# Sparse products of a graph network on one Trainium2 core: a 16-slot gather ring, static index columns, loops of four groups

## The chip, the cores and the metric

The kernel runs on 1 core of one Trainium2 chip. The metric is device time of that core in microseconds: three runs of the kernel before gave 11555.72, 11559.22 and 11560.43 us, median 11559.22 us. One more execution was profiled; all rows below are from it.

## The reference, cut to what matters

Four graph layers run one after the other on 50000 nodes of 128 features and 25000 edges sorted by destination. The change is in the second (L1), which is five sublayers, each with five sparse products on top of one another:

```python
def prop(z):
    return segment_sum(edge_weight[:, None] * z[src], dst, num_segments=N_SUP)
for i in range(5):
    z = h @ W[i] + b[i]
    x_start = prop(z)
    xi = h
    for _ in range(5):
        xi = (prop(xi) + x_start) / (2.0 + GAMA)
    mean, var = jnp.mean(xi, axis=0), jnp.var(xi, axis=0)
    out = gamma[i] * (xi - mean) / jnp.sqrt(var + BN_EPS) + beta[i]
    h = jnp.where(out > 0, out, 0.01 * out)
```

All of its pixels belong to segment 0, so only one row of the result is used in the end; the products still run over all edges. The kernel folds `x_start` into the others, so that there are 5 products in each of 5 sublayers: 25 passes over the edges.

## The kernel before, in words

The 25000 edges are 200 tiles (`T`) of 125 edges, one edge to a partition, partition 0 being kept for a carried sum. Four tiles are a group (`GR`), two groups a half-and-half turn of a loop (`U` = 8 tiles, `IT` = 25 turns). A pass works on a table in HBM that has one row of 128 floats for each edge position, reads it by index, and writes the next pass's table.

For each tile of a pass:
- **GpSimd (POOL)** gathers 128 rows of 512 bytes into slot `j` of `G` by an indirect DMA (L864 in `l1_gather`). `G` has 8 slots. The index column comes from `ridx`, 8 columns that VectorE refills from `gidx` (L936). Each gather carries a wait on the semaphore `s_go`, which has been up since the program's start (`steady`), and at every fourth tile there is a wait on `l_idx` (the columns are there) and on `l_sum` (the group that used these four slots two groups ago has been summed).
- **TensorE (PE)** makes the row of the last, unfinished segment of the tile (L981, a matmul with one column of `lring`), and after VectorE's carry the segment sums of the tile (L995, the mask `M` as weights and `G` as data).
- **VectorE (DVE)**, once per group: the carried row goes through the four tiles in five short operations (`running_sums`, L354 and L356), then `lring` and `ridx` are refilled (L934, L936), the four masks of the next group are made (`edge_mask`, L377), and the group's sums are added to the constant part and left in `Y` (L948). In the last pass of a sublayer (`k == 4`) it copies the sums to `Y` and squares them instead (L943, L945).
- **SyncE (SP)** stores each group of `Y` to the next table (L849, `l1_store`, not in a last pass).
- **ScalarE (ACT)** works only in the last passes (L956), in which PE also makes the transposed sums (L991) and the sums over nodes (L962, L964 in `node_sums`).

The order is set by the engines' own programs and by semaphores. PE's group `g` starts when group `g-1`'s carry (`l_ch`) and mask are there and its gathers have landed (`l_got[j]`, one semaphore for each slot). POOL starts a pass only when all stores of the pass before have landed (`l_tab`). Between two sublayers is a dense stage (`turn_act`, `turn_dve`, `turn_pe`), about 139 us, in which POOL gathers nothing. The sublayer loop is `over_layers`: sublayer 0 is written out, sublayers 1 to 4 are a loop; the programs of the five passes in it are written out one behind the other.

The prediction also speaks of two other places where POOL issues gathers: L397 (first graph layer) and L803 (positions, `PGOT`).

Of the kernel before, what the change touches and what calls it, by code (L numbers as in the profile page):

```python
# [7 lines left out]
P, D = 128, 128  # L31
# [6 lines left out]
TG = T // 2  # L38
TP = T + U
# [14 lines left out]
def build(nc, x0, src, dst, ea, ew, w0, b0, w1, b1, gamma, beta, w2, b2, we, be, coef, linw, linb, asrc, adst, out):  # L54
    assert T * TE == E and IT * U == T and CHUNKS * NJ == NC_ and CHUNKS % 2 == 0
# [30 lines left out]
    with ctx:  # L86
# [39 lines left out]
        G = sb("G", [P, U, D + HEADS])  # L126
# [666 lines left out]
        def positions(pool, c, s, n):  # L793
# [28 lines left out]
        l_w, l_wr, l_col, l_base, l_idx, l_mask, l_lr, l_ch, l_row, l_sum, l_ev, l_xt, l_xc, l_yl, l_sq = (  # L822
            sem("l_" + n) for n in "w wr col base idx mask lr ch row sum ev xt xc yl sq".split())
        l_got = pool_sems("l_got", U)
# [9 lines left out]
        def rounds(l, k):  # L834

            return (l * NL + k) * IT
# [15 lines left out]
        def l1_gather(pool, l, k):  # L852
            r0 = rounds(l, k)
            steady(pool, 16 * rounds(l, k + 1))
            for h in range(2):
                pool.wait_ge(l_tab[h], 16 * rounds(l, k + 1))
            with pool.Fori(0, IT) as i:
                for j in range(U):
                    g = 2 * (r0 + i) + j // GR
                    steady(pool, g + 1)  # L860
                    if j % GR == 0:
                        pool.wait_ge(l_idx, g + 1)
                        pool.wait_ge(l_sum, g + 1)
                    pool.indirect_dma_start(G[:, j, 0:D], None, tab_in(k), bass.IndirectOffsetOnAxis(  # L864
                        ap=ridx[:, j:j + 1], axis=0)).then_inc(l_got[j], 16)
# [58 lines left out]

        def l1_dve(dve, l, k):
            r0 = rounds(l, k)
            last = k == NL - 1
            with dve.Fori(0, IT) as i:
                for h in range(2):
                    g = 2 * (r0 + i) + h  # L930
                    running_sums(dve, g, U * i + GR * h, h, lambda j: G[0:1, j, 0:D],
                                 lambda jj: PS[0:1, CAR, jj, :], carry[:, 0:D], l_row, l_ch)

                    nc.vector.tensor_copy(lring[:, GR * h:GR * h + GR],  # L934
                                          lastc[:, bass.ds(U * i + U + GR * h, GR)]).then_inc(l_lr, 1)
                    nc.vector.tensor_copy(ridx[:, GR * h:GR * h + GR],  # L936
                                          gidx[:, bass.ds(U * i + U + GR * h, GR)]).then_inc(l_idx, 1)
                    for j in range(GR):
                        ins = edge_mask(U * i + GR * (h + 1) + j, GR * (1 - h) + j, wccol)
                    ins.then_inc(l_mask, 1)  # L940
                    dve.wait_ge(l_sum, g + 3)
                    if last:
                        nc.vector.tensor_copy(group_of(Y, h), PS[:, SUM + h, :, :]).then_inc(l_yl, 1)  # L943
                        dve.wait_ge(l_yl, 2 * (IT * l + i) + h + 1)
                        nc.vector.tensor_tensor(SQ[h][:], group_of(Y, h), group_of(Y, h), ALU.mult).then_inc(l_sq, 1)  # L945
                    else:
                        dve.wait_ge(l_tab[h], 16 * (rounds(l, k + 1) + i))
                        nc.vector.tensor_tensor(group_of(Y, h), PS[:, SUM + h, :, :], zt_group(i, h),  # L948
                                                ALU.add).then_inc(l_ev, 1)
# [17 lines left out]
        def l1_pe(pe, l, k):  # L967
            r0 = rounds(l, k)
            last = k == NL - 1
            with pe.Fori(0, IT) as i:  # L970
# [925 lines left out]
```

## Time and profile before

| | us |
|---|---|
| median of three runs | 11559.22 |
| span of the profiled execution | 11598.4 |
| the 25 passes, with the four dense stages between (1326 to 9024) | 7698 |
| busy: PE, DVE, POOL, ACT | 7734.7, 6797.1, 7123.4, 1197.8 |
| granted TensorE clock, mean | 0.659 of 2.4 GHz |

For the profiled execution the page gives the span, from its first to its last instruction, and no time beyond it; the span is 39.2 us (0.34%) longer than the median of the three runs. Durations below are of that one execution and are summed against 11598.4. In a row of the time line the columns are: start in us from the span's beginning, duration in us, engine, line, operation, tiles, count; in brackets the engine's idle time before it and what ended that. "issue" is time in which an engine waited for nothing that the profile shows. For a gather the bar is the time of POOL's own work on it, not the transfer, whose landing has a line of its own.

### The profile page before, as it was taken

The numbers are of one execution on the slowest core, as the hardware profiler recorded it, in microseconds if no ns is written. First come the engines' busy times: TensorE is split into PE (matmuls) and PEld (weight loads), VectorE is DVE, ScalarE is ACT, GpSimd is POOL, SyncE is SP. The second block draws the span as 40 slices with busy tenths as digits, with TensorE's granted clock in tenths as the row PEclk, the third lists the DMA queues.
The fourth block names the chain that finished last, engine by engine and source line by source line (L and its number), as shares of the span: only waits on it lengthen the run. The fifth ranks groups of instructions, "written<-read, shape, count | busy, mean of one in ns | idle before, by whom it ended". The sixth has DMA issues, their size and how long they took to land. (4 is left out here: it accounts for less than half of the span.)

```text
span 11598.4 us, 175759 instructions
## 1 busy us (share of the span) xinstructions
PE 7734.7 (67%) x38121; PEld 5090.7 (44%) x38121; DVE 6797.1 (59%) x24532; ACT 1197.8 (10%) x2596; POOL 7123.4 (61%) x7294
## 2 busy tenths in 40 slices
PE   4633377788777797777877778877779177660090
PEld 2423233357333475333663345743337055560070
DVE  5644655567555576555665556765556666450176
ACT  0122000001000011000010000100000511440005
POOL 5756366663666664666636666456666466766664
PEclk8755555679555697555785556965559578785555
DMA  3133354432444424444334444244543522662106
GB/s 126 44 126 142 91 91 92 92 70 69 92 92 92 90 49 95 91 92 92 61 76 93 92 92 81 58 95 92 91 93 52 178 62 63 174 174 36 24 28 268
DMA packets 1057829, 1076.56 MB, mean 93 GB/s; under 512 B 193805, under 2 KB 913982, under 8 KB 1057648
## 3 DMA queue, kind: packets, MB, share of 16 engines
q0 software_dynamic: 211200, 395.39, 22.0%
q1 hardware_dynamic: 723504, 525.23, 14.3%
q10 hardware_dynamic: 123072, 155.41, 4.3%
q14 instruction: 42, 0.34, 0.0%
q8 instruction: 11, 0.18, 0.0%
HBM read 565.26 MB, written 522.63 MB: 94 GB/s over the span
## 5 line engine op out<-in xcount | busy, mean ns | idle before, releaser
L864 POOL DMA_INDIRECT G<-tab,ridx x5000 | 4746.3, 949 | 3013.2 <-issue 2328.4
L981 PE MATMUL PS<-G,lring 128*1 128x128 f32 x10000 | 2411.0, 361 | 1504.0 <-DMA G<-tab,ridx 1470.1
L356 DVE SCALAR_TENSOR_TENSOR G<-G,whole,PS 1x128 f32<-1x128 f32 (+1 forms) x4050 | 1353.8, 334 | 2568.5 <-PE PS L981 1977.4
L995 PE MATMUL PS<-G,M 128*128 128x128 f32 x10000 | 2780.8, 418 | 45.5 <-DVE G L356 44.0
L995 PEld LDWEIGHTS PS<-G,M 128*128 128x128 f32 x10000 | 2155.6, 274 | 684.6 <-issue 376.4
L981 PEld LDWEIGHTS PS<-G,lring 128*1 128x1 f32 x10000 | 556.1, 85 | 3071.0 <-DMA G<-tab,ridx 2721.0
L377 DVE TENSOR_SCALAR M<-keyrow,keycol,wccol 128x128 f32 (+1 forms) x5004 | 1393.6, 350 | 1.0
L956 ACT COPY big<-PS 128x512 f32 x250 | 146.4, 585 | 7147.2 <-PE PS L991 7147.2
L688 ACT ACTIVATE big<-big,nb,rs 128x128 f32<-128x128 f32 x1564 | 614.8, 479 | 935.4 <-POOL nb L679 911.8
L948 DVE TENSOR_TENSOR Y<-PS,big 128x512 f32<-128x512 f32 x1000 | 679.4, 679 | 0.0
L356 DVE SCALAR_TENSOR_TENSOR carry<-G,whole,PS 1x128 f32<-1x128 f32 (+1 forms) x1350 | 451.2, 334 | 182.0 <-DVE G L356 0.3
L354 DVE COPY G<-carry 1x128 f32<-1x128 f32 (+1 forms) x1350 | 397.8, 295 | 236.9 <-PE PS L981 220.9
L991 PE MATMUL PS<-M,G 128*128 128x128 f32 x2000 | 484.8, 327 | 0.0
L773 PE MATMUL PS<-ones,big 128*128 128x1 f32 (+1 forms) x782 | 171.8, 353 | 361.4 <-ACT big L688 361.4
L991 PEld LDWEIGHTS PS<-M,G 128*128 128x128 f32 x2000 | 328.7, 206 | 101.9 <-issue 37.7
L962 PE MATMUL PS<-ends,Y 128*128 (+1 forms) x2040 | 357.1, 245 | 2.9 <-DVE HT L945 2.9
L1738 PE MATMUL PS<-ident,AL 128*100 128x128 f32 x8 | 2.0, 426 | 520.8 <-DVE AL L1684 520.8
L773 PEld LDWEIGHTS PS<-ones,big 128*128 128x128 f32 (+1 forms) x782 | 169.2, 331 | 364.1 <-ACT big L688 364.1
L962 PEld LDWEIGHTS PS<-ends,Y 128*128 128x128 f32 x2040 | 320.6, 198 | 3.3 <-DVE HT L945 3.3
L660 DVE BATCH_NORM_STATS2 st<-big 128x6 f32<-128x128 f32 x1564 | 314.6, 278 | 4.2
L397 POOL DMA_INDIRECT G<-in_x,ridx x200 | 208.2, 1041 | 156.0 <-DVE ridx L467 93.7
L676 POOL TENSOR_TENSOR rs<-rs,minus_half 128x13 f32<-128x13 f32 (+1 forms) x124 | 297.4, 2399 | 10.3
(387 smaller groups left out, 9973.5 us busy)
## 6 DMA issues: line engine op xcount, KB each, us to landing
tab<-Y SPq DMA_DIRECT2D x1250, 256.0 KB, 3.1
G<-tab,ridx POOLq DMA_INDIRECT x5000, 3.3
big<-agg SPq DMA_DIRECT2D x90, 832.0 KB, 6.4
x<-big ACTq DMA_DIRECT2D x60, 832.0 KB, 3.6
big<-x SPq DMA_DIRECT2D x60, 832.0 KB, 4.8
xt_d<-big ACTq DMA_DIRECT2D x30, 858.0 KB, 7.7
x2n<-big ACTq DMA_DIRECT2D x30, 838.5 KB, 3.5
big<-x2n SPq DMA_DIRECT2D x30, 838.5 KB, 5.3
```

The source lines that it names most:

```text
L354: nc.vector.tensor_copy(row0(j), carried).then_inc(made, 1)
L356: nc.vector.scalar_tensor_tensor(carried if jj == GR else row0(j), row0(j - 1), whole[0:1, bass.ds(tile + jj - 1, 1)], local(jj - 1), ALU. ...
L377: return nc.vector.tensor_scalar(M[:, slot, :], keyrow[:, bass.ds(t * P, P)], keycol[:, bass.ds(t, 1)], weights[:, bass.ds(t, 1)], ALU.is_ ...
L660: ins = nc.vector.bn_stats(st6[0:np_, j, :], V[0:np_, j, :])
L688: ins = nc.scalar.activation(X[0:np_, j, 0:D], V[0:np_, j, :], ACT.Identity, scale=rs[0:np_, s, j:j + 1], bias=nb[0:np_, s, j:j + 1])
L773: ins = nc.tensor.matmul(PS[:, ACC1, 0, 0:1], XN[s][0:np_, j, :], ones[0:np_, 0:1], start=False, stop=False, skip_group_check=True)
L864: pool.indirect_dma_start(G[:, j, 0:D], None, tab_in(k), bass.IndirectOffsetOnAxis(ap=ridx[:, j:j + 1], axis=0)).then_inc(l_got[j], 16)
L948: nc.vector.tensor_tensor(group_of(Y, h), PS[:, SUM + h, :, :], zt_group(i, h), ALU.add).then_inc(l_ev, 1)
L962: nc.tensor.matmul(PS[:, ACC1, 0, 0:2], Y[:, GR * h + j, :], here, start=False, stop=False, skip_group_check=True)
L981: nc.tensor.matmul(PS[0:1, CAR, j % GR, :], lring[:, j:j + 1], G[:, j, 0:D], start=True, stop=True).then_inc(l_row, 1)
L991: ins = nc.tensor.matmul(PS[:, PA + h, j % GR, :], G[:, j, 0:D], M[:, j, :], start=True, stop=True)
L995: ins = nc.tensor.matmul(PS[:, SUM + h, j % GR, :], M[:, j, :], G[:, j, 0:D], start=True, stop=True)
```

## The change

`G` gets 16 slots (`RG`). A pass's 200 gathers are written out (no loop on POOL), each with its own constant column of `gidx`; `ridx`, its refill and `l_idx` go. POOL waits once in 8 gathers, from the 16th on: for the sums of both groups whose slots come next (`l_sum`) and for their carries (`l_ch`). The other 7 gathers of the 8 carry no wait. The loops of PE and DVE have four groups in a turn, 12 turns and two groups written out behind them. The two credits on `l_sum` go, so DVE waits for `g + 1` instead of `g + 3`, which is the same group.

```diff
+RG = 16
+NG = RG // GR
+LI = T // RG
+LREM = (T - LI * RG) // GR
-        G = sb("G", [P, U, D + HEADS])
+        G = sb("G", [P, RG, D + HEADS])
-        l_got = pool_sems("l_got", U)
+        l_got = pool_sems("l_got", RG)
...
         def l1_gather(pool, l, k):
-            r0 = rounds(l, k)
+            g0 = 2 * rounds(l, k)
             steady(pool, 16 * rounds(l, k + 1))
             for h in range(2):
                 pool.wait_ge(l_tab[h], 16 * rounds(l, k + 1))
-            with pool.Fori(0, IT) as i:
-                for j in range(U):
-                    g = 2 * (r0 + i) + j // GR
-                    steady(pool, g + 1)
-                    if j % GR == 0:
-                        pool.wait_ge(l_idx, g + 1)
-                        pool.wait_ge(l_sum, g + 1)
-                    pool.indirect_dma_start(G[:, j, 0:D], None, tab_in(k), bass.IndirectOffsetOnAxis(
-                        ap=ridx[:, j:j + 1], axis=0)).then_inc(l_got[j], 16)
+            for t in range(T):
+                if t >= RG and t % U == 0:
+                    free = g0 + (t - RG) // GR + 2
+                    steady(pool, free, OPS * free + 1)
+                    pool.wait_ge(l_sum, free)
+                    pool.wait_ge(l_ch, OPS * free + 1)
+                pool.indirect_dma_start(G[:, t % RG, 0:D], None, tab_in(k), bass.IndirectOffsetOnAxis(
+                    ap=gidx[:, t:t + 1], axis=0)).then_inc(l_got[t % RG], 16)
...
+        def group_loop(eng):
+            with eng.Fori(0, LI) as i:
+                for q in range(NG):
+                    yield i, q
+            for q in range(LREM):
+                yield LI, q
+
+        def got_before(l, k, slot):
+            return (LI + (1 if slot < GR * LREM else 0)) * (NL * l + k)
...
         def l1_dve(dve, l, k):
-            with dve.Fori(0, IT) as i:
-                for h in range(2):
-                    g = 2 * (r0 + i) + h
-                    running_sums(dve, g, U * i + GR * h, h, lambda j: G[0:1, j, 0:D],
-                                 lambda jj: PS[0:1, CAR, jj, :], carry[:, 0:D], l_row, l_ch)
+            for i, q in group_loop(dve):
+                h, g, tile = q % 2, g0 + NG * i + q, RG * i + GR * q
+                running_sums(dve, g, tile, 0, lambda j, q=q: G[0:1, GR * q + j, 0:D],
+                             lambda jj: PS[0:1, CAR, jj, :], carry[:, 0:D], l_row, l_ch)
...
-                    nc.vector.tensor_copy(ridx[:, GR * h:GR * h + GR],
-                                          gidx[:, bass.ds(U * i + U + GR * h, GR)]).then_inc(l_idx, 1)
...
-                    dve.wait_ge(l_sum, g + 3)
+                dve.wait_ge(l_sum, g + 1)
...
         def l1_pe(pe, l, k):
-            with pe.Fori(0, IT) as i:
-                for h in range(2):
-                    g = 2 * (r0 + i) + h
+            for i, q in group_loop(pe):
+                h, g, tile = q % 2, g0 + NG * i + q, RG * i + GR * q
...
-                        pe.wait_ge(l_got[j], 16 * (r0 + i) + 16)
+                    pe.wait_ge(l_got[s], 16 * (got_before(l, k, s) + i) + 16)
...
-                credit(l_sum, 2)
-                nc.vector.tensor_copy(ridx[:], gidx[:, 0:U]).then_inc(l_idx, 2)
```

The instructions of PE and DVE for a group are otherwise the same, on the same tiles. No other stage of the kernel is touched.

## Rows read from the trace of the kernel before

**Rows 1.** The page: the span, and the gathers of the 25 passes.

```profile
span 11598.4 us, 175759 instructions
...
L864 POOL DMA_INDIRECT G<-tab,ridx x5000 | 4746.3, 949 | 3013.2 <-issue 2328.4
```

**Rows 2.** Busy time by stretch: a middle pass, a last pass, a dense stage.

```profile
core 0: us, PE busy (x) PEld busy (x) DVE busy (x) ACT busy (x) POOL busy (x), PEclk, DMA share, GB/s
...
1613.10:1897.50 284.40, 217.57 (x800) 112.49 (x800) 168.02 (x600) 0.00 (x0) 188.72 (x200) 0.58 0.49 92
...
2467.70:2755.90 288.20, 270.23 (x2020) 232.31 (x2020) 202.52 (x656) 29.27 (x50) 189.55 (x201) 0.92 0.27 46
2755.90:2894.80 138.90, 97.88 (x800) 93.12 (x800) 100.11 (x154) 38.08 (x50) 0.56 (x1) 0.97 0.33 95
```

**Rows 3.** Time line of POOL: gathers 1, 8, 9 and 13 of the first pass.

```profile
1326.48 0.96 POOL L864 DMA_INDIRECT G<-tab,ridx  x1 [125.42 <-issue]
...
1335.24 0.94 POOL L864 DMA_INDIRECT G<-tab,ridx  x1 [0.30 <-issue]
1337.37 0.98 POOL L864 DMA_INDIRECT G<-tab,ridx  x1 [1.18 <-PE PS L995]
...
1342.40 0.94 POOL L864 DMA_INDIRECT G<-tab,ridx  x1 [0.30 <-issue]
```

**Rows 4.** Time line of POOL: the first pass's last gather, and three later heads.

```profile
1600.79 0.94 POOL L864 DMA_INDIRECT G<-tab,ridx  x1 [0.30 <-issue]
1613.10 0.94 POOL L864 DMA_INDIRECT G<-tab,ridx  x1 [11.37 <-issue]
...
2894.84 0.99 POOL L864 DMA_INDIRECT G<-tab,ridx  x1 [138.37 <-issue]
...
8735.39 0.94 POOL L864 DMA_INDIRECT G<-tab,ridx  x1 [10.63 <-issue]
```

**Rows 5.** Time line of all engines, 1760 to 1773: one turn of the ring.

```profile
1761.82 0.94 POOL L864 DMA_INDIRECT G<-tab,ridx  x1 [0.90 <-PE PS L995]
...
1765.57 0.94 POOL L864 DMA_INDIRECT G<-tab,ridx  x1 [0.30 <-issue]
...
1768.93 0.38 PE L981 MATMUL PS<-G,lring 128*1 128x128 f32 x2 [0.61 <-DMA G<-tab,ridx]
...
1769.91 1.71 PE L995 MATMUL PS<-G,M 128*128 128x128 f32 x6 [0.19 <-DVE G L356]
...
1772.42 0.94 POOL L864 DMA_INDIRECT G<-tab,ridx  x1 [0.70 <-issue]
```

**Rows 6.** The gathers' line by itself: durations in ns, landing.

```profile
L864 POOL DMA_INDIRECT G<-tab,ridx x5000: 938/945/1473, 1326.5 to 9009.6; - x193
...
DMA to landing us min/median/max: 2.9/3.3/5.5
```

**Rows 7.** Time line, 1590 to 1595: two carries of DVE with gathers nearly in time.

```profile
1590.54 0.34 DVE L356 SCALAR_TENSOR_TENSOR carry<-G,whole,PS 1x128 f32<-1x128 f32 x1
...
1592.82 0.38 PE L981 MATMUL PS<-G,lring 128*1 128x128 f32 x2 [0.20 <-DMA G<-tab,ridx]
...
1594.79 0.33 DVE L356 SCALAR_TENSOR_TENSOR carry<-G,whole,PS 1x128 f32<-1x128 f32 x1
```

**Rows 8.** Time line, 2604 to 2611, in a last pass: PE's row matmuls of two groups.

```profile
2605.40 1.03 PE L981 MATMUL PS<-G,lring 128*1 128x128 f32 x8
...
2610.28 0.82 PE L981 MATMUL PS<-G,lring 128*1 128x128 f32 x6
```

**Rows 9.** Other gathers of POOL, by shape: busy us, mean ns, idle before.

```profile
L803 POOL DMA_INDIRECT PGOT<-lastpos,PIDX x200 | 237.1, 1186 | 76.0 <-issue 51.9 <-POOL PIDX L798 23.8 <-DMA PGOT<-lastpos,PIDX 0.3
L397 POOL DMA_INDIRECT G<-in_x,ridx x200 | 208.2, 1041 | 156.0 <-DVE ridx L467 93.7 <-issue 55.8 <-DVE Y L490 4.3
```

**Rows 10.** Groups by line in one pass, 1613 to 1890: the index refill.

```profile
L936 DVE COPY ridx<-gidx 128x4 int32 x49 | 9.8, 199 | 0.0
```

**Rows 11.** DMA issues by line: KB each, us to landing.

```profile
wmat<-in_L_gnn_W SPq DMA_DIRECT2D x5, 64.0 KB, 1.9
```

More of the change, by code:

```diff
@@ new lines, in l1_dve @@
+            for i, q in group_loop(dve):
+                h, g, tile = q % 2, g0 + NG * i + q, RG * i + GR * q
+                running_sums(dve, g, tile, 0, lambda j, q=q: G[0:1, GR * q + j, 0:D],
+                             lambda jj: PS[0:1, CAR, jj, :], carry[:, 0:D], l_row, l_ch)
+                nc.vector.tensor_copy(lring[:, GR * h:GR * h + GR],
+                                      lastc[:, bass.ds(tile + U, GR)]).then_inc(l_lr, 1)
+                for j in range(GR):
+                    ins = edge_mask(tile + GR + j, GR * (1 - h) + j, wccol)
+                ins.then_inc(l_mask, 1)
+                dve.wait_ge(l_sum, g + 1)
+                if last:
+                    nc.vector.tensor_copy(group_of(Y, h), PS[:, SUM + h, :, :]).then_inc(l_yl, 1)
+                    dve.wait_ge(l_yl, 2 * IT * l + NG * i + q + 1)
+                    nc.vector.tensor_tensor(SQ[h][:], group_of(Y, h), group_of(Y, h), ALU.mult).then_inc(l_sq, 1)
+                else:
+                    dve.wait_ge(l_tab[h], 16 * (rounds(l, k + 1) + NG // 2 * i + q // 2))
+                    nc.vector.tensor_tensor(group_of(Y, h), PS[:, SUM + h, :, :],
+                                            zt[:, bass.ds(tile * D, GR * D)].rearrange("p (s f) -> p s f", f=D),
+                                            ALU.add).then_inc(l_ev, 1)
@@ L967, in l1_pe @@
         def l1_pe(pe, l, k):
[L968 removed]
+            g0 = 2 * rounds(l, k)
             last = k == NL - 1
[L970 to L1000 removed]
@@ new lines, in l1_pe @@
+            for i, q in group_loop(pe):
+                h, g, tile = q % 2, g0 + NG * i + q, RG * i + GR * q
+                gl = 2 * IT * l + NG * i + q
+                for j in range(GR):
+                    s = GR * q + j
+                    if j == 0:
+                        pe.wait_ge(l_lr, g + 1)
+                        pe.wait_ge(l_ch, OPS * g + 1)
+                    pe.wait_ge(l_got[s], 16 * (got_before(l, k, s) + i) + 16)
+                    nc.tensor.matmul(PS[0:1, CAR, j, :], lring[:, GR * h + j:GR * h + j + 1], G[:, s, 0:D],
+                                     start=True, stop=True).then_inc(l_row, 1)
+                for j in range(GR):
+                    s = GR * q + j
+                    if j == 0:
+                        pe.wait_ge(l_mask, g + 1)
+                        if last and h == 0:
+                            pe.wait_ge(l_xc, gl)
+                    pe.wait_ge(l_ch, OPS * g + j + 2)
+                    if last:
+                        ins = nc.tensor.matmul(PS[:, PA + h, j, :], G[:, s, 0:D], M[:, GR * h + j, :],
+                                               start=True, stop=True)
+                        if j == GR - 1:
+                            ins.then_inc(l_xt, 1)
+                    ins = nc.tensor.matmul(PS[:, SUM + h, j, :], M[:, GR * h + j, :], G[:, s, 0:D],
+                                           start=True, stop=True)
+                ins.then_inc(l_sum, 1)
+                if last:
+                    pe.wait_ge(l_sq, gl)
+                    node_sums(pe, tile - GR, 1 - h)
```

45 lines of the change are left out of this document (4 added, 41 removed).

## The prediction

> **What bounds the kernel now.** The page comes first: 5000 gathers at 949 ns fill 4746 us on POOL, and POOL stood idle another 3013 us ahead of them [rows 1]. No engine is full, so the stretches are next. A middle pass takes 284.4 us, with PE busy 218 us, DVE 168 us and POOL 189 us of it; a last pass takes 288.2 us, a dense stage 138.9 us [rows 2]. The reader is to see that all 25 passes cost much the same, though a last pass has two and a half times as many matmuls. What they share is the gathers.
>
> POOL's time line shows two paces. Where it need not wait, a gather starts 1.249 us after the one before: from 1326.48 to 1335.24 are 7 of them [rows 3]. About once in 8 the gap is longer, 1.18 us instead of 0.30 at 1337.37, ended by PE's sums. The 200 gathers of this pass start between 1326.48 and 1600.79 [rows 3, 4]: 274.31 us for 199 steps, where 199 x 1.249 would be 248.55. So 25.8 us of this pass is waiting for slots.
>
> Why it waits is seen in one turn of the ring [rows 5]. The gather at 1761.82 opens a group and 1765.57 closes it (3.75 us). The last one's data reach PE at 1768.93 (3.36 us; the median landing is 3.3 us [rows 6]). Row matmuls, carry and sums end at 1769.91 + 1.71 = 1771.62 (2.69 us), and 0.80 us later the same slots are gathered again. That is a circle of 10.60 us for 8 gathers whose issue takes 8 x 1.249 = 9.99 us. With 8 slots the latency of the circle is the bound, by a little; POOL's issue is right behind it.
>
> **The change part by part.**
>
> *16 slots.* Gather 16 (counted from 0) waits for tiles 4 to 7, which were gathered 12 issues, 15.0 us, ahead of it; the circle from the first of these to their freed slots is 10.6 us. So 4.4 us are left, and the wait ends before POOL gets there. What goes is all the waiting inside passes. Over all 25 it is the idle time of the gathers' row less what stays. 3013.2 [rows 1] less 125.4 for the first head, 4 x 138.4 = 553.7 for the four behind dense stages (137.9 to 139.3), 212 for the other 20 (10.2 to 11.4 each), of which 11.37, 138.37 and 10.63 stand as examples [rows 3, 4], leaves 2122. Of it 25 x 199 x 0.300 = 1492 is the gap that every gather has. The rest, **630 us**, is the wait; one pass gave 25.8, and 25 times that is 644.
>
> *What is late next.* The gathers themselves, at 4 x 1.249 = 5.00 us for a group. In a middle pass PE and DVE need less: two carries stand 4.25 us apart where one of the gathers was still 0.20 us late [rows 7], so their own chain is at most 4.25. In a last pass PE's row matmuls of two groups start 4.88 us apart, the data being there, with the node sums between them [rows 8]. That too is below 5.00, by only 2.4%, and 16 slots cover its small stalls; I take 10 us in all as lost there (2 us for each of five last passes, 0 to 27 being the ends: all of it hidden, or nothing gained in them at 26 to 30 us of waiting a pass, 135 in all).
>
> *Once in 8, no wait on the other 7.* The gap of 0.30 us is the same for a gather that has only the always satisfied `s_go` ahead of it and for one with the registers and the waits of a new half turn (1342.40, the 13th) [rows 3]. What is satisfied is looked at while the gather ahead still works, so I take 0 for its removal. The trace has no gather without any wait, so the ends are 0 and the whole gap, 5000 x 0.30.
>
> *Static columns.* The gather's index address was constant already. The refill goes: 0.20 us for each group on DVE [rows 10], beside waits for PE; in the tail of each pass it might bring 0.1 us, 2.5 us in all, which I leave out. It was also a releaser of a few gathers, within the 630.
>
> *Loops of four groups.* The same instructions for each group, fewer turns (12 and a rest instead of 25). A turn's own cost is not visible now: gaps at every second group do not differ. I take 0; the ends are a small gain and rival B.
>
> *Heads and tails.* A pass starts when the last store has landed. From the last gather's start to the next pass's first is 12.31 us [rows 4]; landing, two groups' work, store and its landing are all as before, and so are the dense stages. Nothing of the 20 heads goes. POOL now has no loop turn in a pass; its written-out program runs at one instruction or so in 1.2 us.
>
> *Sum.* 11598.4 - 630 + 10 = 10978 us of span. A pass becomes 248.6 + 12 = 261 us. The profiled span is 39.2 us above the median of the runs, so the median to expect is **10940 us** (0.946 of before).
>
> **The rivals.**
>
> A, *a gather without a wait is cheaper.* If a part of the 0.30 us is the wait attached to it, POOL's pace falls below 1.249 us and the middle passes run at up to PE's and DVE's 4.25 us a group. With the whole gap gone: 20 passes x 50 x (5.00 - 4.25) = 750 us, and 5 x 50 x 0.12 = 30 more, to 10160 us. With 0.05 us of it: 7/8 x 5000 x 0.05 = 219, less what the last passes can't use, about 10740. Against it is the equality of the gaps [rows 3]; for it, only that no such gather is in the trace. Chance 0.08.
>
> B, *a turn of the longer loop costs PE and DVE.* Their programs are twice as long in each turn; if a turn's start must be fetched anew, a load from HBM lands in 1.9 us [rows 11]. With 12 turns a pass, and both engines losing one after the other, 3.8 us a turn stands against a cover of 4 x (5.00 - 4.25) = 3.0 in a middle pass and 4 x 0.12 = 0.5 in a last one: 240 x 0.8 + 60 x 3.3 = 390 us, to 11330; with one engine alone 60 x 1.4 = 84, to 11020. The 25 turns now, of which some must lie across any boundary, show nothing. The same range holds the case in which PE can't keep up in the last passes (up to 11065). Chance 0.11.
> The Trainium skill, "Runtime: NRT & Kernel Launch", Instruction fetch mechanics, speaks for B: an engine holds two blocks of 256 instructions, fetched in order, and a taken branch to one outside must wait for a fetch. DVE's 600 instructions a pass [rows 2] are 24 in a turn of 25, with some register work beside them, and 48 in the new turn, so by that rule a turn may still lie inside two blocks; then the time is mine.
>
> C, *slower: the gather itself gets longer.* Its place is POOL's 945 ns [rows 6], which rises if VectorE, busier per us, or the wider index tile holds it up. It decides from 630 / 5000 = 0.126 us a gather. The nearest rows: L397 has 1041 ns on average, +0.092, which would bring back 460 us (11400), and L803 1186 ns, +0.237, which gives 10940 + 1185 = 12125 us [rows 9]. Against it: in these passes the same instruction is 938 at least and 945 in the median, with DVE at 59% of the time [rows 2, 6]; DVE's share goes to 64%. Chance 0.03, half of it beyond 11536.
> The Trainium skill, "DMA: Bandwidth & Descriptors", SWDGE vs HWDGE vs iDMA, names the mechanism: VectorE in its two-port mode shuts GpSimd out of the SBUF in which it writes descriptors. By that rule the stage would grow; this trace's 949 against 945 ns shows 4 ns of it.
>
> **How the numbers follow.** My case has 0.78, A 0.08, B 0.11, C 0.03. Its own range is 10890 to 11010: 1 us more or less in each of 25 tails, 10 ns in the pace of 5000 gathers (50 us), 0 to 27 and somewhat more in the last passes. To 10840 and 11080 it takes in the mild parts of A and B. A measurement of this kernel tells 0.2% from no change (23 us). Faster by more than that: all of the first three and half of C, 0.975, less 0.01 for all else; same 0.01; slower 0.025.
>
> **What would show it right or wrong.** Right: POOL busy stays at 945 ns with gaps of 0.30 us, the "PE PS" releasers leave the gathers' row, its idle time falls to about 2390 us; a middle pass takes 261 us and a last one 262; PE's wait for gathers becomes even, one in every 1.25 us, and POOL's busy share in a pass rises from 66% to 72%. A is right if the gaps are under 0.30. B shows as idle time of DVE or PE by "issue" once in four groups, and POOL waiting for sums again. C shows in the gathers' mean. I am wrong at the root if the gathers still wait for PE in middle passes, or if heads grow beyond 12 us.

## The result, and the profile after

The changed kernel takes **11033.17 us** (median of 4 runs, 11030.04 to 11037.31), the kernel before 11557.47 (4 runs, 11547.94 to 11560.43) beside it: ratio 0.9547 [0.9533, 0.9561], faster by 4.5%. The direction is the predicted one. The time is 93 us above the predicted 10940, inside the stated range (to 11080), and 23 us above what my own case allowed (11010). The profiled execution has a span of 11035.5 us and a time of 11037.31.

The page of the changed kernel, with the gathers and the row matmuls that use them (busy us, mean ns, idle before):

```profile
span 11035.5 us, 168221 instructions
...
PE 7330.5 (66%) x38121; PEld 4969.5 (45%) x38121; DVE 6626.4 (60%) x23280; ACT 1198.1 (11%) x2596; POOL 7177.9 (65%) x7294
...
L844 POOL DMA_INDIRECT G<-tab,gidx x5000 | 4795.3, 959 | 2404.1 <-issue 1421.3
L970 PE MATMUL PS<-G,lring 128*1 128x128 f32 x10000 | 2169.6, 345 | 1302.9 <-DMA G<-tab,gidx 1256.1
```

Against [rows 1] the span is 562.9 us shorter. The gathers' idle time fell by 609 us, and their busy time *rose* by 49, from 949 to 959 ns each. PE now waits for gathers, not POOL for PE.

The gathers' line by itself, with what ended the idle time ahead of them:

```profile
L844 POOL DMA_INDIRECT G<-tab,gidx x5000: 942/948/1467, 1327.4 to 8450.0; - x193
its engine sat idle before it (us, times) until:
  issue: 1421.3, 4650
  DMA tab<-Y: 883.7, 25
  PE PS L985: 55.8, 183
  DVE carry L337: 43.3, 142
...
DMA to landing us min/median/max: 3.0/3.4/5.5
```

What to see: the 25 heads are 883.7 us. The rest of the row is 4975 gaps of 0.305 us each: 55.8 / 183 and 1421.3 / 4650 are both 0.305. So the 55.8 us still put down to PE's sums aren't a wait for them; in those gathers the sums happened to end inside the ordinary gap.

Busy time by stretch: a middle pass with its head, a last pass, a dense stage (columns as in [rows 2]):

```profile
core 0: us, PE busy (x) PEld busy (x) DVE busy (x) ACT busy (x) POOL busy (x), PEclk, DMA share, GB/s
1588.40:1849.50 261.10, 199.74 (x800) 107.79 (x800) 159.90 (x550) 0.00 (x0) 190.62 (x200) 0.66 0.59 101
2371.00:2636.20 265.20, 256.31 (x2013) 223.53 (x2014) 198.50 (x600) 29.32 (x50) 194.35 (x200) 0.96 0.30 50
2636.20:2779.10 142.90, 100.19 (x808) 95.34 (x808) 101.84 (x160) 37.95 (x50) 0.58 (x1) 0.95 0.30 92
```

The middle pass takes 261.1 us where [rows 2] had 284.4. The last one takes 265.2 for 288.2, and shows its cost in the POOL column: 194.35 us for the same 200 gathers. The DMA share is the mean busy share of the core's 16 DMA engines. Counted from the starts of all 5000 gathers, from first to last of a pass (heads left out):

| us | before | after | change over all |
|---|---|---|---|
| middle pass, mean of 20 | 273.3 | 250.7 | -451 |
| last pass, mean of 5 | 275.9 | 255.5 | -102 |
| head between passes, mean of 20 | 11.55 | 11.02 | -11 |
| turn with the dense stage, mean of 4 | 151.9 | 152.6 | +3 |
| before the first gather | 1326.5 | 1327.4 | +1 |
| after the last gather's start | 2588.7 | 2585.5 | -3 |
| span | 11598.4 | 11035.5 | -563 |

All of the gain is inside the passes. 199 steps of 0.959 + 0.305 us would be 251.5 us, and the passes take 250.7 and 255.5: they now run at POOL's issue. Of the 4975 gaps only five are over 0.4 us, all in last passes and 3.5 us in all beyond the usual gap: 0.6 to 0.9 us ahead of the 17th gather of four of the five, and 1.9 us ahead of the second gather of the last one.

### The profile page after: what moved, and what is told of

Same layout as the page of the kernel before. It is cut to its first block and busy times, and to the rows that moved or that the text cites. A ratio compares the mean times of both kernels' runs of the same rounds, so it can differ in the third digit from the quotient of the medians.

```text
span 11035.5 us, 168221 instructions
## 1 busy us (share of the span) xinstructions
PE 7330.5 (66%) x38121; PEld 4969.5 (45%) x38121; DVE 6626.4 (60%) x23280; ACT 1198.1 (11%) x2596; POOL 7177.9 (65%) x7294
## 5 line engine op out<-in xcount | busy, mean ns | idle before, releaser
L844 POOL DMA_INDIRECT G<-tab,gidx x5000 | 4795.3, 959 | 2404.1 <-issue 1421.3
L970 PE MATMUL PS<-G,lring 128*1 128x128 f32 x10000 | 2169.6, 345 | 1302.9 <-DMA G<-tab,gidx 1256.1
L985 PE MATMUL PS<-G,M 128*128 128x128 f32 x10000 | 2636.9, 392 | 86.1 <-DVE G L337 82.8
L985 PEld LDWEIGHTS PS<-G,M 128*128 128x128 f32 x10000 | 1977.2, 252 | 731.1 <-DVE G L337 385.6
L970 PEld LDWEIGHTS PS<-G,lring 128*1 128x1 f32 x10000 | 631.0, 88 | 2587.1 <-DMA G<-tab,gidx 2156.4
L937 DVE TENSOR_TENSOR Y<-PS,big 128x512 f32<-128x512 f32 x1000 | 673.1, 673 | 0.1
L981 PE MATMUL PS<-M,G 128*128 128x128 f32 x2000 | 462.2, 314 | 0.5
L335 DVE COPY G<-carry 1x128 f32<-1x128 f32 (+1 forms) x1350 | 315.2, 234 | 205.1 <-PE PS L970 198.2
```

The lines of the kernel that those rows point to most:

```text
L335: nc.vector.tensor_copy(row0(j), carried).then_inc(made, 1)
L844: pool.indirect_dma_start(G[:, t % RG, 0:D], None, tab_in(k), bass.IndirectOffsetOnAxis(ap=gidx[:, t:t + 1], axis=0)).then_inc(l_got[t % R ...
L970: nc.tensor.matmul(PS[0:1, CAR, j, :], lring[:, GR * h + j:GR * h + j + 1], G[:, s, 0:D], start=True, stop=True).then_inc(l_row, 1)
L981: ins = nc.tensor.matmul(PS[:, PA + h, j, :], G[:, s, 0:D], M[:, GR * h + j, :], start=True, stop=True)
L985: ins = nc.tensor.matmul(PS[:, SUM + h, j, :], M[:, GR * h + j, :], G[:, s, 0:D], start=True, stop=True)
```

## The experiments

Four theories stood after the result. *Ring*: the slots, with the longer loops that come with them, brought nearly all of it, and the pace is now POOL's own. *Every-gather wait*: dropping waits or the static columns brought a part. *Price*: 16 slots made POOL run at its issue, so what a gather costs decides, and one can ask what sets it (rows moved, or a fixed price). *VectorE*: the 49 us come from VectorE's work beside the gathers. No run below separates the slots from the longer loops, since none has one without the other. The kernels of one section ran on one chip, and each is compared with the kernel before on that chip.

### A chip on which TensorE pauses

The first four were the kernel before again; the changed kernel with 8 slots; with the index columns refilled; and with a wait on every gather.

```diff
 ring8
-RG = 16
+RG = 8
-                if t >= RG and t % U == 0:
-                    free = g0 + (t - RG) // GR + 2
+                if t >= RG and t % GR == 0:
+                    free = g0 + (t - RG) // GR + 1
 ridx16
+                if t % GR == 0:
+                    cols = g0 + 2 + max(0, t // GR - 3)
+                    steady(pool, cols)
+                    pool.wait_ge(l_idx, cols)
-                    ap=gidx[:, t:t + 1], axis=0)).then_inc(l_got[t % RG], 16)
+                    ap=rcols[:, t % RG:t % RG + 1], axis=0)).then_inc(l_got[t % RG], 16)
+                    nc.vector.tensor_copy(rcols[:, GR * q:GR * q + GR],
+                                          gidx[:, bass.ds(tile + RG, GR)]).then_inc(l_idx, 1)
 every_wait
+                steady(pool)
                 pool.indirect_dma_start(G[:, t % RG, 0:D], None, tab_in(k), bass.IndirectOffsetOnAxis(
```

Expected of the kernel before again:

> The kernel before, once more. Its profiled execution had a span of 11598.4 us, 39 us above its runs, while the profiled execution of the changed kernel (11035.5 us) lies among its own runs. Theory P (profiling costs nothing, that one execution was long by itself): the new profile has a span of 11545 to 11565 us, and the comparison by stage shows where the 39 us were. Rival Q (the profile of this kernel is always some 40 us longer): 11590 to 11605 us again.

Of 8 slots:

> The changed kernel with 8 slots again, POOL waiting at every fourth tile for the group two groups back; gathers stay written out, with static columns and no other wait; with 8 slots the loops of PE and DVE have two groups in a turn. Theory S (the slots are the whole gain): the circle of 10.6 to 11 us for 8 gathers is back, middle passes of 284 us, 11540 to 11570 us. Rival W (written-out gathers, static columns and the waits taken off the other gathers give part of it): 11100 to 11450 us.

Of refilled columns:

> The changed kernel with a 16-column ring for the indices that VectorE refills once a group, and a wait of POOL for it at every fourth tile; the 16 slots, the written-out gathers and the wait for sums once in 8 stay. Theory S: 11020 to 11055 us, as the changed kernel. Rival W: 50 to 300 us more. Beside that: if reading the index column from the 208-column tile is what made each gather 3 ns longer (947 against 944 ns in the median of the first sublayer), the median is 944 again and the time 15 us less, with some of it back for the refill; if not, it stays 947.

Of a wait on every gather:

> The changed kernel with the wait on the always satisfied semaphore s_go put back on each gather. Theory S and my prediction (a satisfied wait costs nothing): gap between gathers 305 ns, 11033 us within 0.2%. Rival A of the prediction, turned round (the wait is part of the gap, and the change won something by dropping it): gap above 305 ns, 5 us more for each ns, 11080 us or more. If the 3 ns in the gather's own median come from the missing wait, the median is 944 ns here.

This chip was another one, and it overturned all four expectations of time: the kernel before took 13123 us on it (12 runs, 13093.66 to 13153.33), 13.5% more than above, and 13167.81 in the run with a profile. Against that, 8 slots gave 13069.65, ratio 0.9959 [0.9943, 0.9974]; refilled columns with 16 slots 13423.76, 1.0227 [1.0203, 1.0251]; a wait on every gather with 16 slots 13455.99, 1.0244 [1.0217, 1.0272]. On this chip both kernels with 16 slots are *slower* than before.

The trace shows why the passes can't profit. A stretch of the every-gather-wait kernel, all engines:

```profile
1906.29 2.08 PE L986 MATMUL PS<-G,M 128*128 128x128 f32 x8
...
1908.56 0.81 PE L971 MATMUL PS<-G,lring 128*1 128x128 f32 x6 [0.19 <-issue]
...
1910.88 0.94 POOL L845 DMA_INDIRECT G<-tab,gidx  x1 [0.30 <-issue]
1913.72 0.69 DVE L938 TENSOR_TENSOR Y<-PS,big 128x512 f32<-128x512 f32 x1 [4.31 <-remote]
1914.34 0.94 POOL L845 DMA_INDIRECT G<-tab,gidx  x1 [2.52 <-issue]
1914.46 0.21 DVE L335 COPY G<-carry 1x128 f32<-1x128 f32 x1
1914.73 1.97 PEld L986 LDWEIGHTS PS<-G,M 128*128 128x128 f32 x8 [4.44 <-DVE G L335]
```

PE's sums end at 1906.29 + 2.08 = 1908.37, yet VectorE's addition, which by then waits for nothing else (its wait for the store that used `Y` was over at 1908.9), starts at 1913.72. The semaphore events of the trace have the update for these sums at 1913.59, with those of the row matmuls right behind it at steps of 42 ns: the updates came 5.2 us after the end that the profile gives the sums. That end is modelled, so the trace does not tell whether the array had finished or was itself held up; PE went on taking up instructions until 1910.3. The traces of this chip also hold fewer of PE's updates than others (235 in the second pass of this kernel, 675 in that of the changed one), so not each can be followed. It recurs: in the middle passes of the two kernels with 16 slots such a pause comes every 12.2 us, once in 8 tiles, 25 to a pass. With 8 slots the marks of such a pause (updates piled up at steps of 42 ns) are less regular, 12 to 60 us apart. A middle pass takes near 306 us all the same in every kernel tried here (306.1 before, 305.2, 306.3 and 306.6). The waits of that kernel give the sum of it:

```profile
DVE Y L938 <- remote: 1733.6, 440, 11.2
PE PS L986 <- DVE G L335: 1709.6, 421, 11.1
...
POOL G L845 <- PE PS L986: 1097.0, 168, 9.9
```

What makes the time differ are mainly the last passes: 372.5 us before, 361.2 with 8 slots, 411.8 and 411.6 with 16, where VectorE's long waits again come 25 to a pass, every 17 us or so. They are 196 of the 281 us by which the span of the refilled columns exceeds that of the kernel before; heads (14.3 us instead of 11.5) and turns with a dense stage (165 instead of 156) are 92, other stages give a little back. Against other chips all stages are slower here (first gather at 1449 us instead of 1327). Why TensorE's updates pause on this chip, and why 16 slots with the four-group loops make its last passes longer, stays open; the unedited changed kernel didn't run there.

The unit prices could be read nonetheless. With a wait on every gather, a gather that isn't held up follows the one before at a gap of 305 ns (median), with a duration of 947 ns (median); with refilled columns it is 305 and 947; without either, in the kernel after, 305 and 948. So **the attached wait and the columns cost nothing on POOL**. The trace of the change alone decides the same: 4650 gathers ended by "issue", 4400 of them without any wait, at 0.305 us. The Trainium skill, "Perfetto Trace Analysis", DMA Instruction — SWDGE (GPSIMD), has such an instruction wait for its semaphores in a wait queue ahead of the execution FIFOs. This trace agrees with a look that costs the engine nothing: the gap is 305 ns with and without.

### What sets the price of a gather

```diff
 half_rows (rows126: 126 in place of 64)
-                pool.indirect_dma_start(G[:, t % RG, 0:D], None, tab_in(k), bass.IndirectOffsetOnAxis(
-                    ap=gidx[:, t:t + 1], axis=0)).then_inc(l_got[t % RG], 16)
+                pool.indirect_dma_start(G[0:64, t % RG, 0:D], None, tab_in(k), bass.IndirectOffsetOnAxis(
+                    ap=gidx[0:64, t:t + 1], axis=0)).then_inc(l_got[t % RG], 16)
 one_mask
-                for j in range(GR):
+                for j in range(1):
                     ins = edge_mask(tile + GR + j, GR * (1 - h) + j, wccol)
 sq_act (VectorE's square is taken out of its loop; in ScalarE's:)
+                    act.wait_ge(l_yl, 2 * (IT * l + i) + h + 1)
+                    nc.scalar.activation(SQ[h][:], group_of(Y, h), ACT.Square).then_inc(l_sq, 1)
```

The first leaves the upper half of the rows out of every gather and with it half of the edges; the second leaves out two rows that hold no edge, so that nothing is lost (in both the slots are cleared once). The third leaves out three of four masks in each group; the fourth computes all. Half the rows and one mask have a single execution each, no ratio.

> The changed kernel with each gather of the 25 passes fetching 64 rows instead of 128 (the rows of partitions 64 to 127 are left out and stay zero). It prices a row of a gather and shows what bounds next. Theory R (POOL's work is a price per row and a small fixed one): the gather takes 520 to 620 ns, its pace is 0.85 to 0.92 us, below PE's and DVE's own chain, and a middle pass takes 50 x 4.05 to 4.25 + 12 = 215 to 225 us; the gathers wait for PE again. Rival F (a fixed price, whatever the rows): 900 ns or more, passes of 261 us as now.

> The changed kernel with gathers of 126 rows: partitions 126 and 127 hold no edge, their rows of G are zeroed once at the start and have weight 0. Output as the reference's. Theory R (7 ns a row): 15 ns less a gather, 5000 x 0.015 = 75 us less, 10950 to 10970 us. Rival F (fixed price): no change within 0.1%. Rival D (126 rows are spread over fewer DMA engines than 128, so landings get later): landing median above 3.6 us, heads up by as much, 11035 to 11060 us.

> The changed kernel with VectorE making one of the four masks of a group (the other three are left out, their old contents are used). In the changed kernel 100 of 4000 gathers of middle passes took over 1030 ns, all of them beside a mask and the addition after it. Theory V (VectorE's masks hold up POOL's work on a gather): the long gathers of middle passes are gone, their mean falls from 955 to 949 ns or less, about 25 us less in all. Rival U (something else that repeats with the groups, the additions or the stores to the table): the mean stays 954 to 956 ns.

> The changed kernel with the squares of the last passes made by ScalarE from Y instead of by VectorE. In the changed kernel a gather of a last pass takes 975 ns on average against 955 in a middle pass, and two thirds of those over 1030 ns lie beside the square, which reads two operands from SBUF. Theory V2 (that square holds up POOL): last passes' mean falls to 955 to 960 ns, they take 3 to 4 us less each, 15 to 20 us in all: 11010 to 11020 us. Rival U2 (the copies of sums or masks do it): the mean stays above 970 ns, 11025 to 11045 us.

On this chip the kernel before took 11518.97 us (9 runs). Half the rows: 10763.66. Two rows fewer: 11218.89, ratio 0.9742 [0.9729, 0.9755]. One mask of four: 10966.92. The square on ScalarE: 10997.2, ratio 0.9551 [0.9538, 0.9565]. The gathers' rows in this order, and behind them the one-mask kernel's line by itself, for the median:

```profile
L844 POOL DMA_INDIRECT G<-tab,gidx x5000 | 4548.6, 910 | 2374.7 <-issue 1485.9 <-DMA tab<-Y 855.0 <-DVE carry L337 20.4
```

```profile
L844 POOL DMA_INDIRECT G<-tab,gidx x5000 | 4991.1, 998 | 2394.4 <-issue 1424.2 <-DMA tab<-Y 878.6 <-PE PS L985 71.3
```

```profile
L844 POOL DMA_INDIRECT G<-tab,gidx x5000 | 4751.5, 950 | 2385.1 <-issue 1413.7 <-DMA tab<-Y 865.9 <-PE PS L985 61.3
```

```profile
L844 POOL DMA_INDIRECT G<-tab,gidx x5000 | 4770.1, 954 | 2395.7 <-issue 1415.2 <-DMA tab<-Y 876.6 <-PE PS L985 56.4
```

```profile
L844 POOL DMA_INDIRECT G<-tab,gidx x5000: 938/946/1457, 1325.6 to 8384.1; - x193
```

The idle column hardly moves from one kernel to the next, 2375 to 2396 us. Only the first number does, and the time with it. Half the rows have a median of 904 ns where the changed kernel has 947: 43 ns for 64 rows, 0.7 ns a row. **The price of a gather is nearly fixed** (drawn on to no rows at all it would still be 861 ns, an estimate from these two), and leaving bytes out is worth little: half of them save 234 us against the square on ScalarE on this chip. Rival F was right about the gather and theory R wrong; the passes fell to 251 us with their heads, between the two. The pace follows it, as POOL's time line of the half-rows kernel shows:

```profile
1403.83 0.90 POOL L844 DMA_INDIRECT G<-tab,gidx  x1 [0.31 <-issue]
1405.04 0.90 POOL L844 DMA_INDIRECT G<-tab,gidx  x1 [0.30 <-issue]
```

126 rows cost *more* than 128, 988 ns in the median against 947, and the time is 222 us above that of the square on ScalarE on the same chip, which is the 5000 x (998 - 954) ns of their two rows. The landing didn't move (3.3 us), so it isn't the transfer, and none of the three expectations had this. The rows of the DMA queue that carries the gathers show what goes with it (packets, MB, share; half the rows, 126 rows, the square on ScalarE):

```profile
q0 software_dynamic: 211200, 231.55, 10.2%
```

```profile
q0 software_dynamic: 291200, 390.63, 20.9%
```

```profile
q0 software_dynamic: 211200, 395.39, 25.1%
```

126 rows make 80000 packets more, 16 for each of the 5000 gathers, and 64 rows make not one less than 128. Counted in a middle pass, a gather of 128 rows is 16 packets of 4096 bytes and 16 of 4, one of 64 rows is 16 of 2048 and 16 of 4, and one of 126 rows is 14 of 4096, 14 of 512 and 20 small ones. So the price goes with the packets more than with the rows: 42 ns for 16 of them, counting the two rows left out at 0.7 ns, or 2.6 ns each (an estimate), and the 861 ns above hold only for a shape that keeps the 32 packets. That POOL's time goes into the packets is argued from these three shapes; no run changes the packets alone.

Three masks fewer brought the gathers' mean to 950 ns, 7 to 9 less than the changed kernel's on other chips, and the middle pass to 249.5 us, the last to 251.4. In middle passes the mean is 949.0 ns, where the kernel with the square on ScalarE has 953.5 on the same chip. Gathers over 1000 ns are 14 in a thousand here, against 60 to 63 in the changed kernel and 9 in the kernel before, which makes all four masks too. So masks take part in lengthening the gathers, and how they fall beside them decides; the next section has the count. The square on ScalarE brought the last passes to 251.5 us (956 ns a gather instead of 975) and left the middle ones, which have no square, at 250.4.

### The slots alone, and the change again

Since the first chip could not tell what the slots were worth, the 8-slot kernel ran again, beside the unedited changed kernel and the square on ScalarE; no edit is new.

> The changed kernel, once more, beside the kernel before on one chip. On the chip of ring8, ridx16, every_wait and before2 the kernel before took 13123 us and the two versions with 16 slots 1.023 and 1.024 of it; there TensorE's semaphore updates came 5 to 6 us late about once in 12 us. Theory L (that is a trait of that chip): on a chip where the kernel before takes 11500 to 11570 us the changed kernel is at 0.953 to 0.957 of it; on one with the pauses at 1.02 to 1.03. Rival M (the versions with 16 slots lose for a reason of their own somewhere): the ratio is above 1 here too.

> The same kernel as ring8: 8 slots, gathers written out, static columns, POOL waiting at every fourth tile. Theory S on a chip without pauses: middle passes 284 us from head to head, ratio to the kernel before 0.997 to 1.002. Rival W: ratio 0.96 to 0.99. With pauses: 0.996 as before.

> The same kernel as sq_act (squares of the last passes on ScalarE). It took 10997 us and 0.9551 of the kernel before where that took 11519 us. Beside the changed kernel on the same chip: by theory V2 15 to 25 us less, 0.998 of it; by U2 the same within 0.1%.

The kernel before took 11592.08 us here (15 runs, 11583.24 to 11611.17). The changed kernel: 11060.68, ratio 0.9537 [0.9524, 0.955]. With 8 slots: 11567.67, **0.9976** [0.9967, 0.9985]. With the square on ScalarE: 11045.12, 0.9527 [0.9514, 0.954], which is 0.9986 of the changed kernel in the same rounds. It is the fastest complete version: the two intervals overlap, but all five of its runs (11038.08 to 11053.01) lie below all five of the changed kernel's (11054.27 to 11076.24). Theories L, S and V2 hold; M, W and U2 are false. The gathers' rows of these three:

```profile
L844 POOL DMA_INDIRECT G<-tab,gidx x5000 | 4785.6, 957 | 2443.4 <-issue 1434.4 <-DMA tab<-Y 909.0 <-PE PS L985 70.7
```

```profile
L844 POOL DMA_INDIRECT G<-tab,gidx x5000 | 4743.2, 949 | 2980.9 <-issue 1430.8 <-DMA tab<-Y 885.4 <-PE PS L985 645.3
```

```profile
L844 POOL DMA_INDIRECT G<-tab,gidx x5000 | 4769.3, 954 | 2433.4 <-issue 1432.0 <-DMA tab<-Y 905.2 <-PE PS L985 64.8
```

The 8-slot kernel has the static columns and no wait on three of four gathers, with loops of two groups as before, and it still has 645.3 us put down to PE's sums (578 us of waiting beyond the usual gap in all, where the changed kernel has 17 here); its middle pass is 272.5 us, as before (273.3). So of the 46.3 thousandths 43.9 are the slots with the longer loops, and all the rest of the change is 2.4, some 28 us. That of these two it is the slots is argued, not run: 8 slots with four-group loops is missing. The traces tell what the loops could bring there. In middle passes the gather that waits for the first group of a turn of PE's and DVE's loops waits 0.59 us beyond the usual gap, the one that waits for the second 0.29 (kernel before: 0.59 and 0.33). If a turn costs that 0.3 us, half as many turns save 75 us (an estimate), about a seventh of what went. Its gathers are 949 ns, those of the changed kernel 957: 8 ns or 40 us is what the faster pace costs POOL on one and the same chip.

The wait did not go altogether on this chip. 14 gathers of the changed kernel's middle passes still waited for PE's sums, 0.9 to 2.1 us each and 15 us in all, as at 7809.82; the kernel with the square on ScalarE had 11. Behind it are late landings, 4.2 us in the median and 9.9 at most, where 8 slots have 3.3 and 5.7 on the same chip. The second pass of both, the changed kernel first, each with the landings of its gathers, as far as the trace has them:

```profile
1592.30:1855.60 263.30, 199.86 (x800) 110.90 (x800) 159.42 (x550) 0.00 (x0) 189.35 (x200) 0.66 0.90 100
```

```profile
DMA to landing us min/median/max: 2.9/4.2/9.9
```

```profile
7809.82 0.94 POOL L844 DMA_INDIRECT G<-tab,gidx  x1 [2.14 <-PE PS L985]
```

```profile
1612.70:1895.00 282.30, 217.24 (x800) 111.51 (x800) 158.75 (x550) 0.00 (x0) 188.76 (x201) 0.58 0.48 93
```

```profile
DMA to landing us min/median/max: 2.9/3.3/5.7
```

The DMA engines are busy 90% of the pass instead of 48%, for the same bytes at a pace 7% faster: a packet of 4096 bytes takes 963 ns in it instead of 453. On the chip of the result they are at 59% and such a packet takes 535 ns. So here the DMA engines come close to being the bound behind POOL's issue. Why their packets get so much slower on this chip is open.

The long gathers stand beside VectorE. A stretch of a last pass of the changed kernel:

```profile
2620.31 1.10 DVE L358 TENSOR_SCALAR M<-keyrow,keycol,wccol 128x128 f32 x4
...
2620.95 1.02 POOL L844 DMA_INDIRECT G<-tab,gidx  x1 [0.30 <-issue]
...
2622.04 0.69 DVE L934 TENSOR_TENSOR HT<-Y 128x512 f32<-128x512 f32 x1
...
2622.28 1.28 POOL L844 DMA_INDIRECT G<-tab,gidx  x1 [0.30 <-issue]
...
2623.86 0.94 POOL L844 DMA_INDIRECT G<-tab,gidx  x1 [0.30 <-issue]
```

The gather of 1.28 us lies beside the square (L934), the one of 1.02 us beside the masks, and the one that begins under neither takes 0.94. In the middle passes of this second profile all 97 of 4000 gathers over 1030 ns have masks and the addition (L937) beside them; in the last ones 92 of 1000 are that long, 78% of them beside a square. Taken over all middle gathers, those with nothing of this beside them average 947 ns, those beside masks alone 947, beside the addition alone 948, and the 739 beside both 975; in the last passes those beside the square alone average 1090. The kernel before has 564 of the gathers beside both, at 950 ns. So it isn't the masks' time as such that costs here but how a gather falls on them. Which part of VectorE's work does it stays open: on the chip with the pauses, 48 of the 56 long gathers of middle passes (a wait on every gather) lie beside masks without the addition. The Trainium skill, "DMA: Bandwidth & Descriptors", SWDGE vs HWDGE vs iDMA, says that VectorE in its two-port mode shuts GpSimd out of the memory in which it writes descriptors. The traces agree in part: all the long gathers lie beside work of VectorE, but gathers beside masks alone are no longer than others on this chip, and in which mode VectorE ran no trace shows. The size is 8 to 10 ns on average and 19 to 24 in the last passes. In these, fewer masks or no square bring the mean to the same 956 ns, so it is a question of what falls together, not of the sum of VectorE's work.

### A wait at every fourth gather

```diff
-                if t >= RG and t % U == 0:
-                    free = g0 + (t - RG) // GR + 2
+                if t >= RG and t % GR == 0:
+                    free = g0 + (t - RG) // GR + 1
```

> The changed kernel with POOL waiting at every fourth tile, from the 16th on, for the one group whose slots come next, instead of once in 8 for two groups. Theory S (with 16 slots the wait is over before POOL gets to it either way): as the changed kernel, 0.953 to 0.956 of the kernel before, gaps of 305 ns with nothing above it in middle passes. Rival X (the wait for two groups holds POOL back, or waiting once in 8 saves time): ratio below 0.952, or above 0.957. On a chip with TensorE's pauses, where POOL does wait for PE: below the 1.023 of ridx16, if the coarse wait was part of that loss.

It took 11010.69 us, on yet another chip whose kernel before took 11511.97 (7 runs): ratio 0.9563 [0.9547, 0.9579], against 0.9547 and 0.9537 for the changed kernel. Middle passes 250.2 us, last ones 254.2. Its gathers' row:

```profile
L844 POOL DMA_INDIRECT G<-tab,gidx x5000 | 4780.7, 956 | 2399.2 <-issue 1300.9 <-DMA tab<-Y 881.3 <-PE PS L985 121.9
```

About twice the idle time is put down to PE's sums, 121.9 us for 55.8, and the idle time is the same in all. Such a releaser's name in a gap that has its usual length is no wait: no gap of a middle pass is above 0.32 us. The ratio is a little above theory S's 0.956 and short of rival X's 0.957, and its interval overlaps both others, from other chips. With 16 slots it makes no difference that these runs can show how often POOL waits.

One gather for two tiles, with two index columns, would halve the fixed price; it wasn't tried.

## Why the prediction was right, and where it was off

**The circle of 8 slots was the bound, and its wait went.** Right. The cover of 4.4 us held in the runs of the result, of the gather's price and of the wait at every fourth gather: no gather of a middle pass waits there. On the chip on which the change ran again, landings of up to 9.9 us used it up 14 times, for 15 us in all; the prediction had taken the landing as fixed. The circle and the pace named in it give nearly the whole change: without the slots and the longer loops only 2.4 of 46.3 thousandths are left. Those 2.4 were predicted as nothing. So was a turn of the loop ("gaps at every second group do not differ"), but in the kernel before the gather that waits for a turn's first group waits 0.59 us beyond the usual gap, that for its second 0.33.

**The 630 us.** The step that subtracted 25 x 199 gaps of 0.300 us took a rounded figure of the time line. The gap is 0.305, as the prediction's own pace and median would have given (1.249 less 0.945 is 0.304): 25 us of the 630 were no wait, and the wait was 605. (The seven steps that it names give 1.251 us, since the first is a long one; 1.249 is the usual step of that time line.)

**"The gathers themselves" at 1.249 us a step.** Here the largest term failed: the sum left POOL's durations at what they were. They rose from 949 to 959 ns, 49 us over 5000. On one chip with and without the slots it is 957 against 949, 40 us. In the profile of the result some 15 us of the 49 are another thing: its floor is 942 ns instead of 938 and its medians are 3 ns up, which no other profile of 128 rows has. That is rival C at a thirteenth of its deciding 126 ns. The 4 ns between mean and median that the prediction took for this cost are only in part that: gathers with nothing of VectorE's beside them average 947 ns in the kernel before, 2 less than all. The mechanism had been named and given 0.03 as a case that reverses the result, when it should have been a term with a price of its own: a faster pass sets VectorE's masks beside other phases of a gather.

**The 10 us lost in the last passes.** Predicted as stalls of PE. These are 3.5 us in all, five gaps; the other gaps are 0.305 us too. The last passes do lose, through gathers of 975 ns: 255.5 us instead of 250.7, 24 us in all, of which 20 are in the 49.

**Heads and other stages.** Predicted unchanged: -11, +3, +1 and -3 us, near enough. By windows the middle pass came out at 261.1 (predicted 261) and the last one at 265.2 (262). That the 261 fits so well is luck: it is 248.6 + 12, and the means of 20 are 250.7 + 11.0, one term 2 us too small and the other 1 too large. POOL's share (190.62 / 261.1 = 73%, predicted 72%) was right; VectorE's is 61%, not 64. The "PE PS" releasers did not leave the gathers' row as forecast (55.8 us, 183 gathers), though none of that is waiting.

**The sum and its base.** In spans 10978 was predicted and 11035.5 measured, 57 us more: 25 + 49, less 7 of the last passes' term and 10 for heads and stages, to rounding. The rest of the 93 us is the last step, which took 39.2 us off because the profiled execution of the kernel before lay that much above the median of the runs. For the changed kernel span and median differ by 2.3 us, so 37 us of the error are this step; without it 10978 + 57 would have met the 11033 measured. What the surplus was stays open. The profiled execution of the kernel before lies 41 us above its median here and 43 on the chip with the pauses, as rival Q had it, that of the 8-slot kernel 1 and those of the changed one 2 and 14. A surplus of waiting for slots would go with the slots, and to take it off again counts it twice; but the medians of the kernel before differ as much from one occasion to the next (11512, 11519, 11557 and 11592 us), so it may as well be the chip. The offset belonged into the range, not into the sum. That the measured time still lies in the range is in part luck: its end at 11080 had been opened for mild cases of A and B, and neither came.

**The rivals.** A (a gather without a wait is cheaper) is false: 305 ns with and without. B (turns of the longer loop, or PE unable to keep up) is false where TensorE doesn't pause: the gathers' gaps show none of it, and PE waits for gathers. That a turn's start is not fetched anew shows in the queues of the page of the changed kernel that carry instructions:

```profile
q14 instruction: 114, 0.93, 0.0%
q8 instruction: 19, 0.31, 0.0%
```

These are 133 packets in the whole program, while PE and DVE have 300 turns each in the passes. The Trainium skill, "Runtime: NRT & Kernel Launch", Instruction fetch mechanics, cited beside B, has only a taken branch to a block that isn't held wait for a fetch; the trace agrees with a turn that lies within what is held. On the chip with the pauses the last passes with 16 slots are 40 us longer than before, which can't be fetches either (119 + 19 packets in the kernel with a wait on every gather); it stays open. C is true in its direction, and small.

## What to carry to other kernels

A ring that is short by a few per cent makes every turn wait; count the circle (issue, landing, use, free) against slots times issue, look at what share of the time the DMA engines are busy, since a landing can grow with the pace, and when the wait goes, the producer's own instruction becomes the whole price. Then look at that instruction's mean, not its median or minimum, and expect it to grow a little, since a faster pace sets it beside other work. A releaser's name beside a gap of the usual length is no wait, and a profile's surplus of some tenths of a per cent over the median is a width of the forecast, not a term of it.

## What the runs showed of the hardware that was not expected

- An indirect gather of 512-byte rows costs POOL 944 ns in the median for 128 rows in three of the five sublayers, 900 to 902 for 64, and 987 or 988 for 126, with 305 ns to the next one. 128 and 64 rows are 32 packets, 126 are 48.
- The same gather takes 952 and 955 ns in the second and third sublayer, in every kernel with 128 rows, and 944 in the first, fourth and fifth (in the one execution with the higher floor 955, 958 and 947); with 126 rows it is 987 or 988 in all of them. What differs isn't known.
- On one chip the same gathers at a pace 7% faster kept the DMA engines busy 90% of a middle pass instead of 48%, and landed 4.2 us after their issue in the median instead of 3.3.
- On one chip of those used TensorE's semaphore updates came some 5 us late again and again, with 16 slots every 12.2 us in middle passes; the kernel before took 13123 us on it, and 11512 to 11592 on four occasions elsewhere. There two kernels with the deeper ring took 2.3 and 2.4% longer than the kernel before.
